# A four-layer Mamba stack with an FP4 feed-forward on one core: TensorE's work laid out anew over the slots, gates and row statistics moved off VectorE, the first norm and the weight preparation moved into the start of the Mamba block

## The chip, the cores and the metric

The kernel runs on one NeuronCore of a Trainium2 chip. The metric is the time of one execution on the device in microseconds, the median of several. Five engines work side by side and meet only at semaphores: TensorE (PE, matrix products into PSUM), VectorE (DVE), ScalarE (ACT), GpSimd (POOL, which reads and writes SBUF only) and SyncE (SP, which issues all DMAs here). Each engine takes its instructions strictly in the order in which the program lists them, so an instruction that waits holds up all behind it.

## The reference

The input x is 4 sequences of 2048 rows of 256 numbers. The layer is a residual Mamba stack of four layers, then a feed-forward with FP4 quantisation:

```python
x = x + mamba_stack(layernorm(x))        # 4 layers, below
x = x + ffn_fp4(layernorm(x))            # H=256, I=704

def mamba_layer(x):                      # D_MODEL 256, D_INNER 512, D_STATE 16
    xs, z = split(x @ in_w.T)
    xc = silu(conv4(xs) + cb)            # causal, 4 taps
    dt, B, C = split(xc @ xp_w.T)        # 16 + 16 + 16
    delta = softplus(dt @ dt_w.T + dt_b)
    h_t = h_{t-1} * exp(delta * A) + (delta * xc) * B     # 512 channels x 16 states
    y = sum_states(h_t * C) + xc * D_skip
    out = (y * silu(z)) @ out_w.T
    return layernorm(out + x) * ln_w + ln_b

def ffn_fp4(x):   # every operand quantised to E2M1 by blocks of 16
    return q(silu(q(x) @ q(w_gate).T) * (q(x) @ q(w_up).T)) @ q(w_down).T
```

All arithmetic is float32.

## The kernel before

The 8192 rows are cut into 16 chunks of 512 time steps, four chunks to a sequence. Three blocks run one after the other, with a barrier of all engines between them. `normalise_input` takes the chunks one by one: load, VectorE's statistics and normalisation, store to the buffer `xbuf` in HBM. `mamba_layers` makes 64 turns, one for each chunk of each layer (turn g is chunk g mod 16 of layer g div 16). `fp4_ffn` first quantises and transposes its weights, then goes over the chunks.

A turn has 16 slots. A slot s holds 512 of the 8192 recurrences (a group, "G" in the code): four states of one tile of 128 channels-by-states, each of them 512 time steps long. In the code of one turn each engine has its own list of what it does in slot s, and this list is the schedule:

- VectorE does four scans (`scan`, L950: h = dA * h + bu along time) and two products (`times_b`, L935: bu = durep * B_all, in PSUM). In slot s the order is scan 0, `times_b(s,1)`, scan 1, scan 2, `times_b(s+1,0)`, scan 3. So `times_b` of the next slot is the second product of this one. Between them it does the gates (`gate`, L956: sz = acc * sz, in slots 2, 6, 10 and 14, after scan 0) and the row statistics of the layer norm (`statistics` in slot 8, `moments` in slot 9).
- TensorE does `broadcast_b(s+1)` (L455, which spreads B over the partitions into the one PSUM tile `B_all`; it waits until both products of slot s have read it), then `sum_states(s-2)` (L473: the sum over states of hc into the one PSUM tile `acc`, preceded by `skip_term` when a tile of channels begins), then the projections of this slot: `project_x` in 2, `project_dt` in 3 and 4, `project_out` in 5 and 6, `project_in` of z in 8 and 9, the transposes of the chunk after next in 10, `project_in` of xs in 11 and 12, `convolve` in 13 to 15 and 0. These all pass through two PSUM tiles W0 and W1, which ScalarE empties.
- ScalarE copies the last states of slot s-1 (`keep_states`, L612, which waits for the last scan of that slot), makes the four decay factors of slot s+1 (`exp`, L603, into `dA`, a ring of 8 tiles), then does its share of the slot: `copy_conv` and `tanh_xc` and `silu_z` in 0 and 1, `copy_proj` in 3, `delta_linear` in 4 and 5, `sigmoids` in 5, `polynomial` in 6, `copy_out` in 6 and 7, `copy_z` in 9 and 10, and so on.
- GpSimd does `times_c` (L832, hc = h * C, two pairs in a slot; pair k waits for scans 2k and 2k+1, and for `acc` to have summed the pair that lay in its buffer two slots before), and as extra work `silu_xc` before slot 2, `softplus` 0 before slot 7, `softplus` 1 after slot 8, 2 after slot 10, 3 after slot 11, the layer norm's small steps in slots 10 and 12, and its weights (`affine`) after slot 15.

A channel of the next turn goes through ScalarE's `sigmoids` and `polynomial`, GpSimd's four softplus steps, a store to HBM (`store_delta`, `store_du`) and a load that repeats it over partitions (`load_delta` into `drep`, `load_du` into `durep`).

The turns are a loop of four over the middle of the 64:

```python
def turns(eng, turn):
    turn(0, 0)
    turn(1, 1)
    with eng.Fori(0, (TOT - 4) // 4) as i:
        for r in range(2, 6):
            turn(4 * i + r, r % 4)
```

In one of four turns (ph 0, the first chunk of a sequence) the scans start from zero, in the others from `carry`.

## Time and profile before

| | before |
|---|---|
| median of 3 runs | 8526.1 us (8520.08 to 8530.0) |
| profiled execution, its own time | 8524.19 us |
| span of its instructions | 8522.4 us |
| busy: VectorE | 7936.9 us, 93% |
| busy: GpSimd | 6990.0 us, 82% |
| busy: TensorE | 6497.0 us, 76% |
| busy: ScalarE | 5407.2 us, 63% |
| granted TensorE clock, mean | 0.9 |

Busy time is the union of an engine's instructions. The shares are means over three blocks with different limits. A wait row says which engine's work ended an idle time of another. In the rows below a matrix product in float32 counts as two instructions ("x2").

### The profile page before, as it was taken

The page shows a single profiled execution, that of the slowest core. Times are in us where ns is not written, and L with a number is a line of the kernel's source. Part 1 is how long each engine was busy: PE and PEld are TensorE (multiplying, and loading weights), DVE is VectorE, ACT ScalarE, POOL GpSimd, SP SyncE. Part 2 cuts the span into 40 slices and gives each one's busy share as a digit, 9 for nine tenths or more (in the row PEclk, how much of TensorE's full clock was granted, in tenths as well). Part 3 has the DMA queues.
Part 4 walks back from the last instruction along what each step waited for, and adds up shares of the span by engine and source line. Part 5 has one row for each costly group of instructions (what it writes and reads, how often), then busy time and mean ns, then how long its engine had stood idle before and what let it go on. Part 6 is the DMA issues. An engine that isn't in the chain of part 4 may idle for free. (4 is left out here: it accounts for less than half of the span.)

```text
span 8522.4 us, 96647 instructions
## 1 busy us (share of the span) xinstructions
PE 6497.0 (76%) x21028; PEld 2513.0 (29%) x21028; DVE 7936.9 (93%) x8028; ACT 5407.2 (63%) x8725; POOL 6990.0 (82%) x3390
## 2 busy tenths in 40 slices
PE   3778777777777777877778777777777777764888
PEld 1222222222222222222222222222222222221555
DVE  3999999999999999999999999999999999995777
ACT  2666666666676666667666666666666666752444
POOL 1888888888888898888888888988888888884555
PEclk9899998988998899889899898989898988986999
DMA  4455443445444544445444454544554444541110
GB/s 134 98 117 120 116 115 97 114 119 132 112 104 111 121 115 113 107 117 123 118 114 112 101 118 115 121 117 107 117 119 117 112 106 106 124 112 43 37 38 30
DMA packets 567641, 909.46 MB, mean 107 GB/s; under 512 B 58288, under 2 KB 202032, under 8 KB 565936
## 3 DMA queue, kind: packets, MB, share of 16 engines
q1 hardware_dynamic: 566960, 902.24, 44.1%
q8 instruction: 201, 3.29, 0.2%
q14 instruction: 480, 3.93, 0.2%
HBM read 715.36 MB, written 186.65 MB: 106 GB/s over the span
## 5 line engine op out<-in xcount | busy, mean ns | idle before, releaser
L832 POOL TENSOR_TENSOR hc<-h,crep 128x1024 f32<-128x1024 f32 x2048 | 4785.2, 2361 | 837.0 <-PE acc L473 755.7
L950 DVE TENSOR_TENSOR_SCAN h<-dA,carry,bu 128x512 f32<-128x512 f32 x3072 | 3769.8, 1266 | 94.3 <-issue 51.8
L935 DVE TENSOR_TENSOR bu<-durep,B_all 128x1024 f32<-128x1024 f32 x2048 | 2485.6, 1214 | 192.1 <-DMA durep<-du_dram 142.5
L603 ACT ACTIVATE dA<-drep,cur 128x512 f32<-128x512 f32 x4096 | 2618.7, 710 | 13.9 <-DMA drep<-delta_dram 13.8
L455 PE MATMUL B_all<-dtc,spread_b 128*128 128x512 f32 x2048 | 1352.2, 747 | 1646.5 <-DVE bu L935 1645.0
L612 ACT COPY carry<-h 128x4 f32<-128x4 f32 x1023 | 201.0, 197 | 2232.2 <-DVE h L950 2184.8
L473 PE MATMUL acc<-hc,gather 128*32 128x512 f32 x8192 | 1279.9, 701 | 4.4 <-POOL hc L832 4.4
L950 DVE TENSOR_TENSOR_SCAN h<-dA,bu 128x512 f32<-128x512 f32 x1024 | 1197.0, 1206 | 9.0 <-ACT dA L603 8.9
L493 PE MATMUL work<-xT,inw 128*128 128x512 f32 x2048 | 1020.2, 643 | 59.5 <-ACT xT L623 48.9
L455 PEld LDWEIGHTS B_all<-dtc,spread_b 128*128 128x128 f32 x2048 | 366.8, 212 | 2330.2 <-DVE bu L935 2266.2
L503 PE MATMUL work<-xs,taps 128*128 128x512 f32 x2048 | 965.2, 614 | 0.0
L493 PEld LDWEIGHTS work<-xT,inw 128*128 128x128 f32 x2048 | 400.6, 207 | 756.1 <-issue 652.1
L503 PEld LDWEIGHTS work<-xs,taps 128*128 128x128 f32 x2048 | 376.6, 194 | 617.6 <-issue 617.6
L531 PE MATMUL work<-outw,sz 128*128 128x256 f32 x2048 | 490.5, 383 | 0.0
L473 PEld LDWEIGHTS acc<-hc,gather 128*32 128x32 f32 x8192 | 173.0, 116 | 972.3 <-issue 686.1
L844 POOL TENSOR_TENSOR quad<-quad,xs 128x2048 f32<-128x2048 f32 x64 | 289.4, 4523 | 154.2 <-ACT quad L701 154.2
L531 PEld LDWEIGHTS work<-outw,sz 128*128 128x128 f32 x2048 | 395.6, 193 | 55.9
L837 POOL TENSOR_TENSOR xc<-xc,quad 128x2048 f32<-128x2048 f32 x64 | 290.0, 4531 | 144.8 <-ACT quad L668 144.8
L1258 PE MATMUL f_gu<-f_wguT,f_xqT 128*128 128x512 f32 (+1 forms) x768 | 341.7, 598 | 72.8 <-ACT f_xqT L1345 65.9
L462 PE MATMUL acc<-xc,skip 128*128 128x512 f32 x512 | 337.6, 749 | 0.0
L854 POOL TENSOR_TENSOR relu<-za,xc 128x2048 f32<-128x2048 f32 x64 | 290.5, 4539 | 0.1
L850 POOL TENSOR_TENSOR za<-quad,relu 128x2048 f32<-128x2048 f32 x64 | 290.0, 4531 | 0.1
(166 smaller groups left out, 6683.6 us busy)
## 6 DMA issues: line engine op xcount, KB each, us to landing
drep<-delta_dram SPq DMA_DIRECT2D x1024, 256.0 KB, 6.0
durep<-du_dram SPq DMA_DIRECT2D x1024, 256.0 KB, 6.7
crep<-c_dram SPq DMA_DIRECT2D x1024, 64.0 KB, 6.4
delta_dram<-za SPq DMA_DIRECT2D x64, 1024.0 KB, 4.3
du_dram<-relu SPq DMA_DIRECT2D x64, 1024.0 KB, 5.3
x_in<-xbuf SPq DMA_DIRECT2D x65, 512.0 KB, 3.9
x_res<-xbuf SPq DMA_DIRECT2D x64, 512.0 KB, 3.9
xbuf<-x_res SPq DMA_DIRECT2D x64, 512.0 KB, 5.6
```

The costliest lines, as they stand in the source:

```text
L455: pe.matmul(B_all[:], spread_b[:, s % QS, :], dtc[:, p_, :], start=True, stop=True).then_inc(bb_ready, 1)
L462: pe.matmul(acc[:], skip[:, q, :], xc[:, p_, q, :], start=True, stop=False, skip_group_check=True)
L473: ins = pe.matmul(acc[32 * k:32 * k + 32, :], gather[:], hc[:, 4 * (s % 2) + k, :], start=False, stop=s % QS == QS - 1, skip_group_check=True)
L493: ins = pe.matmul(W[b][:], inw[:, k, z * DI + e * P:z * DI + (e + 1) * P], xT[:, k, :], start=k == 0, stop=k == KD - 1)
L503: ins = pe.matmul(W[b][:], taps[:, 4 * e + k, :], xs[:, e, k:k + T], start=k == 0, stop=k == 3)
L531: ins = pe.matmul(half, sz[:, p_, k, t * P:(t + 1) * P], outw[:, k, :], start=False, stop=k == DB - 1)
L603: act.activation(dA[:, 4 * (s % 2) + k, :], drep[q % 2][:, k, :], ACT.Exp, scale=cur[:, p_, 4 * s + k:4 * s + k + 1]).then_inc(da_ready, 1)
L832: pool.tensor_tensor(hc[:, pair, :], h[:, pair, :], crep[:, j:j + 1, :].to_broadcast([P, 2, T]), ALU.mult).then_inc(hc_ready, 1)
L854: pool.tensor_tensor(relu[:], za[:], xc[:, p_], ALU.mult).then_inc(du_ready, 1)
L935: dve.tensor_tensor(bu[:, 2 * k:2 * k + 2, :], durep[q % 2][:, 2 * k:2 * k + 2, :], B_all[:].unsqueeze(1).to_broadcast([P, 2, T]), ALU.mul ...
L950: dve.tensor_tensor_scan(h[:, r, :], dA[:, r, :], bu[:, k, :], start, ALU.mult, ALU.add).then_inc(scanned, 1)
L1258: ins = pe.matmul(gu[:, at:at + width], xqT[:, t % 2, k, :], wguT[:, k, at:at + width], start=k == 0, stop=k == KD - 1)
```

## The change

Eight things are changed together.

1. `normalise_input` is gone as a block. Its work is done at the start of the Mamba block: all 16 chunks are loaded into tiles that are still unused (`held`), VectorE works on them in five batches, and the first chunk goes to TensorE straight from there.
2. The quantisation and transposition of the feed-forward's weights is done there too, in five pieces (`quantise_piece` on VectorE, `turn_piece`, `copy_piece`); the result is stored in HBM and loaded when the feed-forward begins.
3. The gates: ScalarE copies `acc` to SBUF (`take_sums`) after the factors in slots 2, 6, 10 and 14, and GpSimd multiplies (`gate`) after `times_c` of these slots. TensorE's next tile of sums waits for ScalarE's copy.
4. The row statistics: ScalarE's `copy_out` gives row sums, its `squares` (slot 10) sums of squares, GpSimd's `mean` (slot 8) and `variance` (slot 11) do the rest. `copy_out` is in slots 7 and 8, `root_guess` in 12, `newton_step` in 13, `normalise` in 15, `affine` after slot 0 of the next turn.
5. The ring of decay factors `dA` has 6 tiles; the other two (`sums`) hold the copies of `acc`. So factor k of slot s+1 waits for the scan six before it: factor 2 for scan 0 of slot s, factor 3 for scan 1.
6. TensorE: the skip term comes after sums, not before (`SKIP_AT`), `project_out` is in quarters over slots 5, 6 and 7 (two in 7), z's third and fourth tiles are in 9 and 10 (`copy_z` in 9, 10 and 11), the taps run in reverse.
7. All 64 turns are written out; there is no loop.
8. A constant in the work on A is changed by 3e-6.

```diff
+    SKIP_AT = (1, 0, 0, 2)
+        sums = dA[:, 6:8, :]
         def turns(eng, turn):
-            turn(0, 0)
-            turn(1, 1)
-            with eng.Fori(0, (TOT - 4) // 4) as i:
...
+            for g in range(TOT):
+                turn(g, g % 4)
             def sum_states(at, p_):
                 n, s, G = at
-                if s % QS == 0:
-                    skip_term(n, p_, s // QS)
+                q = s // QS
+                if s % QS == 0 and positive(DB * n + q):
+                    pe.wait_ge(acc_read, DB * n + q)
...
+                if s % QS == SKIP_AT[q]:
+                    skip_term(n, p_, q)
...
-                        if s in (5, 6):
+                        if s in (5, 6, 7):
                             project_out(g - 1, other, s - 5)
+                        if s == 7:
+                            project_out(g - 1, other, 3)
                     if not is_last(g):
-                        if s in (8, 9):
-                            project_in(nxt, 2 * (s - 8), 1)
-                            project_in(nxt, 2 * (s - 8) + 1, 1)
+                        if s == 8:
+                            project_in(nxt, 0, 1)
+                            project_in(nxt, 1, 1)
+                        if s in (9, 10):
+                            project_in(nxt, s - 7, 1)
@@ ScalarE
-                    if positive(4 * G + k - 7):
-                        act.wait_ge(scanned, 4 * G + k - 7)
-                    act.activation(dA[:, 4 * (s % 2) + k, :], drep[q % 2][:, k, :], ACT.Exp,
+                    if positive(4 * G + k - 5):
+                        act.wait_ge(scanned, 4 * G + k - 5)
+                    act.activation(dA[:, (4 * G + k) % 6, :], drep[q % 2][:, k, :], ACT.Exp,
+            def take_sums(n, q):
+                act.wait_ge(summed, 2 * (NG * n + QS * (q + 1)))
...
+                act.copy(sums[:, q % 2, :], acc[:]).then_inc(acc_read, 1)
+            def squares(m):
+                act.wait_ge(mean_ready, m + 1)
...
+                for t in range(NT):
+                    ins = act.activation(sums[:, t // 2, t % 2 * D:(t % 2 + 1) * D], x_res[:, t, :], ACT.Square, bias=minus_mean[:, t:t + 1],
+                                         accum_out=sq_sum[:, t:t + 1])
                 for s in range(NG):
                     keep_states(group(g, s - 1))
                     exp(group(g, s + 1), here if s + 1 < NG else other)
+                    if s == 10 and not is_first(g):
+                        squares(g - 1)
+                    if s == 2 and not is_first(g):
+                        take_sums(g - 1, DB - 1)
+                    if s in (6, 10, 14):
+                        take_sums(g, (s - 6) // 4)
@@ GpSimd
+            def gate(n, p_, q):
...
+                pool.wait_ge(acc_read, DB * n + q + 1)
+                pool.tensor_tensor(sz[:, p_, q, :], sums[:, q % 2, :], sz[:, p_, q, :], ALU.mult).then_inc(gated, 1)
                     times_c(group(g, s))
+                    if s == 2 and not is_first(g):
+                        gate(g - 1, other, DB - 1)
+                    if s in (6, 10, 14):
+                        gate(g, 1 - other, (s - 6) // 4)
...
-                        if s == 15:
-                            affine(g - 1, 0)
-                            affine(g - 1, 1)
+                    if s == 0 and isinstance(g, int) and g >= 2:
+                        affine(g - 2, 0)
+                        affine(g - 2, 1)
@@ VectorE
                     scan(at, ph, 0)
-                    if s == 2 and not is_first(g):
-                        gate(g - 1, other, DB - 1)
-                    if s in (6, 10, 14):
-                        gate(g, here, (s - 6) // 4)
                     times_b(at, 1)
                     scan(at, ph, 1)
                     scan(at, ph, 2)
                     times_b(nxt, 0)
-                    if s == 9 and not is_first(g):
-                        dve.wait_ge(stats, g)
                     scan(at, ph, 3)
-                    if not is_first(g):
-                        if s == 8:
-                            statistics(g - 1)
-                        if s == 9:
-                            moments()
```

On TensorE, slot 6 of a middle turn stands so before (the broadcast for slot 7, the skip term and sums of slot 4, two quarters of the output projection, the broadcast for slot 8; `acc_read` is given by VectorE's gate):

```order
L455 MATMUL B_all<-dtc,spread_b 128x512 [waits bu_ready]
L462 MATMUL acc<-xc,skip 128x512 [waits acc_read]
L473 MATMUL acc<-hc,gather 32x512 [waits hc_ready]
...
L529 MATMUL work<-x_res,ident 128x256 [waits w_read1]
L531 MATMUL work<-outw,sz 128x256 x4
L529 MATMUL work<-x_res,ident 128x256
L531 MATMUL work<-outw,sz 128x256 x4
L455 MATMUL B_all<-dtc,spread_b 128x512 [waits bu_ready]
```

and so in the changed kernel:

```order
L457 MATMUL B_all<-dtc,spread_b 128x512 [waits bu_ready]
L474 MATMUL acc<-hc,gather 32x512 [waits hc_ready,acc_read]
...
L462 MATMUL acc<-xc,skip 128x512
L537 MATMUL work<-x_res,ident 128x256
L539 MATMUL work<-outw,sz 128x256 x4
L457 MATMUL B_all<-dtc,spread_b 128x512 [waits bu_ready]
```

The skip term moved behind the sums, one quarter moved to slot 7, and the wait for `acc_read` stands on the first sum, between the two broadcasts as before. It is ScalarE that gives `acc_read` now, in slots 5 and 6 of its own list. Before:

```order
L682 ACTIVATE za<-work,bias_now 128x512 [waits w_filled0]
L683 ACTIVATE relu<-work,bias_now 128x512
L686 ACT_TABLE_LOAD
L689 ACTIVATE za<-za,minus_ln 128x2048 [waits w_read1,w_read0]
L691 ACTIVATE xs<-za 128x2048 [waits z_of_dt]
L692 ACT_TABLE_LOAD
L612 COPY carry<-h 128x4 [waits scanned]
L603 ACTIVATE dA<-drep,cur 128x512 [waits scanned] x4
L698 ACTIVATE quad<-xs,quad_bias 128x2048 [waits delta_ready,zz_ready]
```

and in the changed kernel, where the copy of the sums stands behind the two table loads, the two wide steps and the factors of slot 7:

```order
L716 ACTIVATE za<-work,bias_now 128x512 [waits w_filled0]
L717 ACTIVATE relu<-work,bias_now 128x512
L720 ACT_TABLE_LOAD
L723 ACTIVATE za<-za,minus_ln 128x2048 [waits w_read1,w_read0]
L725 ACTIVATE xs<-za 128x2048 [waits z_of_dt]
L726 ACT_TABLE_LOAD
L646 COPY carry<-h 128x4 [waits scanned]
L637 ACTIVATE dA<-drep,cur 128x512 [waits scanned] x4
L755 COPY dA<-acc 128x512 [waits squared,gated,summed]
L732 ACTIVATE quad<-xs,quad_bias 128x2048 [waits delta_ready,zz_ready]
```

What moved is the release of `acc`: from VectorE, after the first scan of the slot, to this place of ScalarE's list.

## Rows read from the trace of the kernel before

**Rows 1.** Busy: PE, PEld, DVE, ACT, POOL; granted clock, DMA share, GB/s; middle turns.

```profile
400.00:2400.00 2000.00, 1552.70 (x5019) 568.63 (x5016) 1944.53 (x1829) 1342.94 (x2152) 1745.64 (x797) 0.91 0.48 115
```

**Rows 2.** Waits: who waited for whom, us in total, times, longest.

```profile
DVE bu L935 <- DMA durep<-du_dram: 142.5, 36, 101.7
...
DVE h L950 <- issue: 51.8, 8, 6.7
...
DVE bu L935 <- PE B_all L455: 46.2, 78, 1.3
```

**Rows 3.** Timeline of VectorE, one slot from zero and one from carry: start, duration.

```profile
300.29 1.21 DVE L935 TENSOR_TENSOR bu<-durep,B_all 128x1024 f32<-128x1024 f32 x1
...
307.00 1.22 DVE L935 TENSOR_TENSOR bu<-durep,B_all 128x1024 f32<-128x1024 f32 x1
...
4619.90 1.21 DVE L935 TENSOR_TENSOR bu<-durep,B_all 128x1024 f32<-128x1024 f32 x1
...
4626.85 1.21 DVE L935 TENSOR_TENSOR bu<-durep,B_all 128x1024 f32<-128x1024 f32 x1
```

**Rows 4.** Timeline of VectorE, first product and last scans of the block.

```profile
214.69 1.23 DVE L935 TENSOR_TENSOR bu<-durep,B_all 128x1024 f32<-128x1024 f32 x1 [101.69 <-DMA durep<-du_dram]
...
7740.53 3.63 DVE L950 TENSOR_TENSOR_SCAN h<-dA,carry,bu 128x512 f32<-128x512 f32 x3
```

**Rows 5.** Timeline of ScalarE, slots 1, 5 and 6 of one turn.

```profile
4575.67 0.20 ACT L612 COPY carry<-h 128x4 f32<-128x4 f32 x1 [3.58 <-DVE h L950]
...
4586.23 1.28 ACT L775 ACT_TABLE_LOAD   x1
...
4604.32 0.20 ACT L612 COPY carry<-h 128x4 f32<-128x4 f32 x1 [1.99 <-DVE h L950]
...
4615.95 2.56 ACT L603 ACTIVATE dA<-drep,cur 128x512 f32<-128x512 f32 x4
4618.41 1.99 ACT L698 ACTIVATE quad<-xs,quad_bias 128x2048 f32<-128x2048 f32 x1
```

**Rows 6.** Groups by line: busy us, mean ns; then idle before.

```profile
L832 POOL TENSOR_TENSOR hc<-h,crep 128x1024 f32<-128x1024 f32 x2048 | 4785.2, 2361 | 837.0 <-PE acc L473 755.7 <-DVE h L950 79.8
...
L710 ACT COPY x_res<-work 128x512 f32<-128x512 f32 x128 | 72.2, 564 | 33.6 <-PE work L531 33.6
...
L1476 POOL TENSOR_TENSOR f_res<-f_res,f_x 128x256 f32<-128x256 f32 x60 | 44.0, 733 | 0.2 <-issue 0.2
```

**Rows 7.** Timeline of TensorE, slots 2 to 8 of that turn.

```profile
4590.23 3.70 PE L510 MATMUL work<-xc,xpw 128*128 128x512 f32 x8
...
4606.64 2.08 PE L455 MATMUL B_all<-dtc,spread_b 128*128 128x512 f32 x2 [2.91 <-DVE bu L935]
...
4614.55 1.02 PE L455 MATMUL B_all<-dtc,spread_b 128*128 128x512 f32 x2
...
4617.35 0.70 PE L529 MATMUL work<-x_res,ident 128*128 128x256 f32 x2
...
4621.78 1.02 PE L455 MATMUL B_all<-dtc,spread_b 128*128 128x512 f32 x2
...
4630.12 1.93 PE L473 MATMUL acc<-hc,gather 128*32 128x512 f32 x8
```

**Rows 8.** Timelines of GpSimd (softplus 0) and VectorE, end of one turn.

```profile
735.76 4.51 POOL L844 TENSOR_TENSOR quad<-quad,xs 128x2048 f32<-128x2048 f32 x1 [2.69 <-ACT quad L701]
...
792.86 1.23 DVE L935 TENSOR_TENSOR bu<-durep,B_all 128x1024 f32<-128x1024 f32 x1 [1.28 <-DMA durep<-du_dram]
```

**Rows 9.** Timelines: start of the kernel, of the Mamba block, of the feed-forward.

```profile
8.01 1.38 DVE L111 TENSOR_SCALAR n_x<-n_x,n_mean,n_root 128x256 f32<-128x256 f32 x4
...
112.89 1.94 PE L483 MATMUL work<-ident,x_in 128*128 128x128 f32 x8 [112.89 <-DMA x_in<-xbuf]
...
7786.06 0.06 DVE L1518 MEMSET f_minus_magic<- 128x1 f32 x1 [12.56 <-PEq L134]
...
7842.65 1.41 DVE L1506 BATCH_NORM_STATS2 f_stats<-f_xa 128x6 f32<-128x256 f32 x4 [3.87 <-POOL f_xa L1417]
```

536 lines of the change are left out of this document (308 added, 228 removed).

## The prediction, made before the changed kernel ran

> **What bounds the kernel now.** First I read the busy shares by window: in 2000 us of middle turns VectorE is busy 97%, GpSimd 87%, TensorE 78%, ScalarE 67% [rows 1]. So VectorE sets the pace. Then its timeline, for what a slot costs when nothing is late. A slot has two products and four scans, and every second product row starts one slot later: 6.71 us in turns from zero, 6.95 us in turns from carry [rows 3]. A turn of 16 slots is 107.4 or 111.2 us, on the mean 110.25 us, and 64 turns are 7056 us. The block takes 7744.2 - 214.7 = 7529.5 us from the first product to the end of the last scan [rows 4], 117.65 us a turn. The 473 us above the bare time are gates, statistics and waits. The waits are short and of three kinds: for durep, whose 142.5 us hold 101.7 us of the start; for the instruction stream at the end of the loop's body ("issue", up to 6.7 us each); for B_all, 46.2 us in 78 waits [rows 2]. The last kind is small, but it shows that the broadcast has little room, and the change acts there.
>
> **The room of the broadcast.** Slot 5 of the turn that I follow starts at about 4604.2 (ScalarE's copy follows at once [rows 5]). TensorE gets B_all back at 4606.6 [rows 7], 2.4 us into the slot; the product that needs the next broadcast starts 4.65 us into a slot (two scans and a product behind the first). Whatever TensorE has queued ahead of the broadcast must be done some 3.6 us into the slot, and what is later stops VectorE one for one.
>
> **The change part by part.**
>
> *Removed from VectorE:* gates and statistics. With every wait gone too, the 473 us would all be won: that is the most that the turns can give.
>
> *The ring of six.* Factor 3 of the next slot now waits for scan 1 of this one, which ends about 3.6 us into the slot (two scans and a product); before, it started at about 2.1 us (three of four factors that take 2.56 us together [rows 5]). So ScalarE is 1.5 us later wherever it isn't already behind.
>
> *ScalarE's copy of the sums.* I take it at 0.56 us, the copy of the same size from PSUM [rows 6]. Its size is not the point; its place is. TensorE's sums of slot 4 wait for it in TensorE's slot 6, ahead of the broadcast for slot 8. ScalarE before: slot 5 starts at 4604.3, and the factors of slot 7 start at 4615.95 [rows 5], behind two table loads and two wide steps, 11.6 us later; with 1.5 us for the ring 13.1, which is 6.2 us into slot 6. Then four factors (2.5 us) and the copy: 9.3 us into slot 6, 2.4 us into slot 7. TensorE was ready at 3.4 us into slot 6, so it idles 6 us. What it still has to do: sums and skip term, 2.8 us less the 1.0 us of the broadcast in the same stretch = 1.8 us; one quarter of the output projection, half of 4.43 = 2.2 us; the broadcast, 1.0 us [rows 7]. That is 5.0 us, and 7.4 us into slot 7 without any loss of clock.
>
> *The clock behind an idle time.* After 2.91 us of idleness the broadcast took 2.08 us in place of 1.02 us, and in slot 8 the sums 1.93 us where they take about 1 us [rows 7]: the lower of the two clock levels. The first steps after such a gap lose 1 us each, for one to three steps. I take 2.2 us a gap, bounds 0 and 3.
>
> So there are three stops of VectorE in a turn, by the same arithmetic:
>
> - A, slot 7: 7.4 + 2.2 - 4.65 = 5.0, and about 0.5 more for waits between steps: 5.5 us (bounds 3.3 and 6.5).
> - B, slot 3. ScalarE's slot 1 starts at 4575.7, its last table load ends at 4587.5 [rows 5]: 11.85, with the ring 13.4, then factors and copy 3.2: 16.6, or 2.7 us into slot 3. Behind it TensorE has the sums (1.0), project_x (3.70) and the broadcast (1.0) [rows 7]: 8.4 + 2.2 - 4.65 = 6.0 us (bounds 3.8 and 7).
> - C, slot 11. In slot 10 the four squares, which the trace doesn't show, stand between the factors and the copy. I take 2.1 us, a quarter of a wide step (1.99 us for 2048 columns [rows 5]) and a little each, between 2.0 us and 3 us. The copy comes at 4.2 + 2.1 + 0.6 = 7 us. Sums, skip term and one half of what was 3.7 us of z follow, and the transposes wait for copy_z in ScalarE's slot 11. The broadcast is done about 7.6 us into slot 11: 3.0 us (bounds 1.9 and 4).
>
> Together 14.5 us a turn, bounds 9.0 and 17.5. In slot 14 the copy is at 4.8 us and costs nothing. Over 63 turns that is 913 us (567, 1100), so the block takes 7056 + 913 = 7970 us, 440 us more than now.
>
> *GpSimd.* It is busy 1745.64 of 2000 us [rows 1], 102.7 us a turn, of which 74.8 us are times_c. Four gates come on. A product of 512 columns lies between the 0.733 us of 256 and the 2.361 us of 1024 [rows 6]; by the line between them 1.25 us each, 5.0 us a turn, and 0.5 us of small steps: 108.2 us against 110.25 us. It fits on the sum but not everywhere: softplus 0 waits for three wide steps (2 us each [rows 5]) that now stand behind the copy, and starts about 8.2 us into slot 7. From softplus 0 to the product of the next turn that needs durep it took 792.9 - 735.8 = 57.1 us [rows 8]; with a gate and small steps 58.8. That ends 67.0 us after slot 7 starts, and VectorE would be there at 8 x 6.95 + 4.65 = 60.25 us. These 6.75 us are hidden by A and C (8.5 us). If A and C weren't there they would come out; the same holds for a 2.5 us stop in slot 3, where affine after slot 0 makes silu_xc, and so project_x, late.
>
> *The loop.* At the end of each of the loop's 15 bodies the engines wait for instructions, up to 6.7 us on VectorE [rows 2]: at most 100 us of the 473 us. Written-out turns have no such place, and I count none, since the bare slot has none; if the long straight list stalled as often, 100 us would come on top, 8920 us. The Trainium skill has the rule (Runtime: NRT & Kernel Launch, Instruction fetch mechanics): prefetch is sequential, a taken branch can stall it, so full unrolling is preferred. It speaks for the change, and the loop's waits agree; what 64 turns in a straight list do, no row here shows.
>
> *The start.* The first product comes 101.8 us after TensorE's first transpose, and all of that chain stays [rows 4, 9]. The transpose waits for the 16 chunks now; the first one alone is normalised at 9.4 us [rows 9]. 9.4 + 101.8 = 111.2, and 4 us for ScalarE's waits for later batches: 115 against 214.7, so -99 us (bounds -110 and -75). Its cover: VectorE has 16 x 2.8 us of statistics and normalisation (1.41 + 1.38 us a chunk [rows 9]), an estimated 15 us of small steps, and the weights, under 56.6 us with all other engines' steps between (I take 40): some 100 us, just under the 115.
>
> *The feed-forward.* From its first instruction to its first statistics are 56.6 us [rows 9]; what stays is the load of x and one sum of 1024 columns (2.36 us [rows 6]), some 9 us by my estimate. -47 us (bounds -50 and -40).
>
> *The tail* of the block: squares for statistics and one more step on each side, +3 us.
>
> **Sum**, against the profiled execution's own 8524.2 us (the median of the runs is 8526.1, so nothing to convert): 8524.2 - 99 - 47 + 3 + 440 = 8821 us. I give 8820. With 9.0 us a turn it is 8475, with 17.5 us 9010. The stops decide the sign: at 9.8 us a turn the times are equal.
>
> **The rivals.**
>
> - *Faster (12%).* The copies come in time, because ScalarE is less behind than the rows put together say, and GpSimd keeps up: 1 us of stops a turn. 7056 + 63 - 7529.5 - 143 + 8524.2 = 7970 us. For it: VectorE is the bound at 97%, and its gates and statistics go. Against it: the trace already shows ScalarE at the factors of slot 7 only 11.6 us behind the start of slot 5, 4.7 us into slot 6, before anything is added. It decides the sign from 9.8 us a turn down.
> - *Only GpSimd's chain and durep (13%).* TensorE's wait for the copy costs little, but softplus 0 is late: 6.75 + 2.5 = 9.25 us a turn, 8490 us. For it: durep is already a wait at the end of many turns [rows 2, 8]. Against it: the sums are queued ahead of the broadcast.
> - *Worse (10%).* GpSimd at 98% of the bare turn falls behind as well (its times_c waits for the sums that wait for ScalarE), and the gaps don't overlap: 19 us a turn, 9110 us.
> - *My forecast (65%)*: 8820 us, own range 8620 to 8980.
>
> Range 8450 to 9000: it takes in the second rival and the forecast's bounds, and leaves out most of the first and the last. Three runs before lie within 10 us, so 0.2% (17 us) is about what can be told. Slower: forecast, worse rival and a little of the second, 0.76. Faster: the first rival and most of the second, 0.20. Within: 0.04.
>
> **What the new profile would show.** Right: VectorE waiting for B_all at the second product of slots 3, 7 and 11, 3 to 6 us each, some 190 long waits with 800 to 950 us; TensorE waiting for ScalarE's copy ahead of these; the first product at 115 us; the feed-forward some 690 us long; VectorE's busy share under 90%; more TensorE time at the lower clock. Wrong: waits for B_all under 200 us in total, or VectorE's longest waits on durep (second rival) or on hc (last rival); statistics or the first product later than 140 us.

## The result, and the profile of the changed kernel

| | kernel before | changed kernel |
|---|---|---|
| median of the runs, us | 8525.2 (8520.1 to 8530.0) | 9100.2 (9094.3 to 9103.2) |
| ratio, 95% interval | 1 | 1.0676 (1.0659 to 1.0693) |
| profiled execution, span us | 8522.4 | 9101.4 |
| predicted, us | | 8820 (8450 to 9000) |

The changed kernel is 6.8% slower. The direction was forecast, and the time lies 100 us above the top of the range.

I read the same views as before. First the busy shares of 2000 us of middle turns (columns as in [rows 1]):

```profile
2400.00:4400.00 2000.00, 1470.50 (x4588) 542.10 (x4588) 1722.20 (x1492) 1312.51 (x2251) 1683.26 (x812) 0.87 0.44 105
```

VectorE is busy 86%, where it was 97% [rows 1]: it lost its gates and statistics and gained more waits than these were worth. The granted clock of TensorE fell from 0.91 to 0.87. Then the waits (who waited for whom: us in total, times, longest):

```profile
POOL hc L932 <- PE acc L474: 1197.4, 463, 9.0
...
DVE bu L1057 <- PE B_all L457: 1100.5, 252, 6.3
ACT dA L637 <- DVE h L1072: 1005.4, 774, 5.6
PE acc L474 <- ACT dA L755: 941.0, 255, 6.0
```

VectorE waits 1100.5 us for the broadcast, 252 times, where it waited 46.2 us [rows 2]. 252 is four in a turn, and I had forecast three. TensorE's sums (L474) wait 255 times for ScalarE's copy (L755): this is the chain that I had described. Now one turn from carry, VectorE's stops at the second product of slots 3, 7, 11 and 13 (start, duration, in brackets the idle time before):

```profile
1062.25 1.23 DVE L1057 TENSOR_TENSOR bu<-durep,B_all 128x1024 f32<-128x1024 f32 x1 [5.82 <-PE B_all L457]
...
1095.84 1.23 DVE L1057 TENSOR_TENSOR bu<-durep,B_all 128x1024 f32<-128x1024 f32 x1 [5.51 <-PE B_all L457]
...
1127.70 1.23 DVE L1057 TENSOR_TENSOR bu<-durep,B_all 128x1024 f32<-128x1024 f32 x1 [3.95 <-PE B_all L457]
...
1144.04 1.23 DVE L1057 TENSOR_TENSOR bu<-durep,B_all 128x1024 f32<-128x1024 f32 x1 [2.33 <-PE B_all L457]
```

In the turn from zero that follows they are 6.21, 6.01, 4.75 and 2.34 us. Over all turns the waits for B_all ahead of these four products are 357.9, 345.5, 255.0 and 139.8 us, which is 5.7, 5.5, 4.05 and 2.2 us a turn. TensorE ahead of the stop in slot 7:

```profile
1080.91 1.12 PE L457 MATMUL B_all<-dtc,spread_b 128*128 128x512 f32 x2 [0.22 <-DVE bu L1057]
1087.90 1.93 PE L474 MATMUL acc<-hc,gather 128*32 128x512 f32 x8 [5.87 <-ACT dA L755]
1089.77 2.08 PE L462 MATMUL acc<-xc,skip 128*128 128x512 f32 x2
1091.63 1.06 PE L537 MATMUL work<-x_res,ident 128*128 128x256 f32 x2
1092.49 2.40 PE L539 MATMUL work<-outw,sz 128*128 128x256 f32 x8
1094.73 1.02 PE L457 MATMUL B_all<-dtc,spread_b 128*128 128x512 f32 x2
1095.68 1.07 PE L474 MATMUL acc<-hc,gather 128*32 128x512 f32 x8
1096.67 0.70 PE L537 MATMUL work<-x_res,ident 128*128 128x256 f32 x2
1097.21 1.89 PE L539 MATMUL work<-outw,sz 128*128 128x256 f32 x8
```

It is idle 5.87 us until the copy, then does sums, skip term and a quarter of the output projection, then the broadcast, and 0.1 us behind that VectorE goes on. The sums take 1.93 us where those behind the broadcast take 1.07, the ident product 1.06 against 0.70, the quarter 2.40 against 1.89, and the skip term 2.08 against the 1.12 of elsewhere: 2.7 us lost behind this idle time. The granted clock has a mean of 0.59 from 1087.9 to 1094.7 us, most of it at the lower of the two levels, and of 1.00 in the 5.3 us that follow. And ScalarE there:

```profile
1083.43 1.28 ACT L726 ACT_TABLE_LOAD   x1
1084.72 0.20 ACT L646 COPY carry<-h 128x4 f32<-128x4 f32 x1
1084.83 2.55 ACT L637 ACTIVATE dA<-drep,cur 128x512 f32<-128x512 f32 x4
1087.29 0.56 ACT L755 COPY dA<-acc 128x512 f32<-128x512 f32 x1
```

It doesn't wait in these steps; it is behind, with the table loads and wide steps of slot 5. The fourth stop, which I had not forecast, begins on ScalarE in slot 12, in three engines' rows:

```profile
1136.44 0.20 POOL L971 TENSOR_TENSOR ve<-ve,c_eps 128x4 f32<-128x4 f32 x1
...
1136.67 0.20 ACT L769 ACTIVATE lnv<-ve 128x4 f32<-128x4 f32 x1 [2.33 <-POOL ve L971]
...
1137.11 1.07 ACT L674 COPY xs<-work 128x512 f32<-128x512 f32 x2
...
1137.74 5.40 PE L500 MATMUL work<-xT,inw 128*128 128x512 f32 x8 [3.16 <-ACT xs L674]
```

The logarithm waits 2.33 us for GpSimd's variance, which stands there behind a gate, a softplus step and two products; the copies of xs are queued behind the logarithm, TensorE's next projection waits 3.16 us for them and then takes 5.40 us in place of 3.70, and the broadcast stands behind it.

The ends, to be laid beside [rows 4, 9]: first product, last scans, start and first statistics of the feed-forward:

```profile
132.83 1.23 DVE L1057 TENSOR_TENSOR bu<-durep,B_all 128x1024 f32<-128x1024 f32 x1 [7.68 <-DMA durep<-du_dram]
...
8359.41 3.61 DVE L1072 TENSOR_TENSOR_SCAN h<-dA,carry,bu 128x512 f32<-128x512 f32 x3
...
8406.95 0.06 DVE L1634 MEMSET f_minus_magic<- 128x1 f32 x1 [43.93 <-PEq L79]
...
8415.51 1.40 DVE L1622 BATCH_NORM_STATS2 f_stats<-f_xa 128x6 f32<-128x256 f32 x4 [8.38 <-POOL f_xa L1542]
```

The start gives 81.9 us (214.7 to 132.8). The block, from the first product to the end of the last scan, takes 8363.0 - 132.8 = 8230.2 us, 700.7 us more than before: 128.6 us a turn, of which 110.25 are the bare turn of the prediction. The other 18.35 us a turn are 1174 us: 1098 us are the four stops, 24 us other waits, and 52 us show as no wait (VectorE's steps and the short gaps between them take 111.1 us a turn here, not 110.25). The step to the feed-forward is 43.9 us (before 41.9), the feed-forward 694.5 us (before 736.3). Together that is 579 us more, the difference of the two spans.

### The profile page after: what moved, and what is told of

It is laid out like the page before. It is cut to its first block and busy times, and to the rows that moved or that the text cites. A ratio compares the mean times of both kernels' runs of the same rounds, so it can differ in the third digit from the quotient of the medians.

```text
span 9101.4 us, 76141 instructions
## 1 busy us (share of the span) xinstructions
PE 6684.8 (73%) x21028; PEld 2597.8 (29%) x21028; DVE 7710.2 (85%) x7155; ACT 5761.2 (63%) x9845; POOL 7299.8 (80%) x3700
## 5 line engine op out<-in xcount | busy, mean ns | idle before, releaser
L932 POOL TENSOR_TENSOR hc<-h,crep 128x1024 f32<-128x1024 f32 x2048 | 4784.0, 2358 | 1343.5 <-PE acc L474 1197.4
L1057 DVE TENSOR_TENSOR bu<-durep,B_all 128x1024 f32<-128x1024 f32 x2048 | 2476.2, 1209 | 1113.6 <-PE B_all L457 1100.5
L637 ACT ACTIVATE dA<-drep,cur 128x512 f32<-128x512 f32 x4096 | 2703.0, 713 | 1007.1 <-DVE h L1072 1005.4
L474 PE MATMUL acc<-hc,gather 128*32 128x512 f32 x8192 | 1272.0, 696 | 946.5 <-ACT dA L755 941.0
L457 PE MATMUL B_all<-dtc,spread_b 128*128 128x512 f32 x2048 | 1218.0, 679 | 855.7 <-DVE bu L1057 851.1
L500 PE MATMUL work<-xT,inw 128*128 128x512 f32 x2048 | 1111.3, 687 | 220.5 <-ACT xs L674 184.5
L510 PE MATMUL work<-xs,taps 128*128 128x512 f32 x2048 | 942.1, 603 | 0.7 <-ACT xs L674 0.7
L500 PEld LDWEIGHTS work<-xT,inw 128*128 128x128 f32 x2048 | 435.3, 223 | 938.2 <-issue 603.1
L474 PEld LDWEIGHTS acc<-hc,gather 128*32 128x32 f32 x8192 | 170.6, 114 | 1825.1 <-ACT dA L755 1225.0
L539 PE MATMUL work<-outw,sz 128*128 128x256 f32 x2048 | 538.3, 410 | 0.0
L539 PEld LDWEIGHTS work<-outw,sz 128*128 128x128 f32 x2048 | 434.0, 212 | 75.1
L462 PE MATMUL acc<-xc,skip 128*128 128x512 f32 x512 | 408.7, 891 | 0.0
L1400 PE MATMUL f_gu<-f_wguT,f_xqT 128*128 128x512 f32 (+1 forms) x768 | 346.9, 605 | 73.7 <-ACT f_xqT L1480 66.7
L517 PE MATMUL work<-xc,xpw 128*128 128x512 f32 x512 | 339.6, 822 | 12.8 <-POOL xc L943 12.8
L939 POOL TENSOR_TENSOR sz<-dA,sz 128x512 f32<-128x512 f32 x256 | 326.6, 1276 | 0.0
```

The costliest lines, as they stand in the source:

```text
L457: pe.matmul(B_all[:], spread_b[:, s % QS, :], dtc[:, p_, :], start=True, stop=True).then_inc(bb_ready, 1)
L462: pe.matmul(acc[:], skip[:, q, :], xc[:, p_, q, :], start=False, stop=False, skip_group_check=True)
L474: ins = pe.matmul(acc[32 * k:32 * k + 32, :], gather[:], hc[:, 4 * (s % 2) + k, :], start=s % QS == 0, stop=s % QS == QS - 1, skip_group_c ...
L500: ins = pe.matmul(W[b][:], inw[:, k, z * DI + e * P:z * DI + (e + 1) * P], xT[:, k, :], start=k == 0, stop=k == KD - 1)
L510: ins = pe.matmul(W[b][:], taps[:, 4 * e + k, :], xs[:, e, k:k + T], start=k == 3, stop=k == 0)
L517: ins = pe.matmul(W[0][:], xpw[:, k, :], xc[:, p_, k, :], start=k == 0, stop=k == DB - 1)
```

## The experiments

All times are medians; the kernel before ran beside each group at 8521 to 8523 us. "Per turn" is a difference of two times divided by 64. A stop's sum is that of VectorE's waits for B_all ahead of the second product of its slot, over all turns. Where rows of a wait are shown, the columns are as above.

### Undoing one thing in the changed kernel

**e1.** ScalarE's copy, and GpSimd's gate behind it, one slot earlier. The squares share the copy's tile, so they now wait for the gate of slot 9.

```diff
-                    if s in (6, 10, 14):
-                        take_sums(g, (s - 6) // 4)
+                    if s in (5, 9, 13):
+                        take_sums(g, (s - 5) // 4)
```

> The changed kernel with ScalarE's copy of the sums, and GpSimd's gate behind it, one slot earlier each (slots 1, 5, 9, 13 in place of 2, 6, 10, 14); the work is the same. Theory of the place (the copy stands behind ScalarE's late factors, TensorE's sums wait for it, the broadcast waits for them): the stops at slots 3, 7 and 11, some 15.3 us a turn, go, TensorE's wait for the copy falls from 941 us to under 100 us; what GpSimd's chain hid behind them comes out, up to 6.75 us a turn, and the stop of 2.3 us in slot 13 stays. Time 9100 - 63 x (15.3 - 6.75) = 8560 us, between 8200 (nothing comes out) and 8650. Rival, GpSimd: its four gates a turn are too much for it, and the waits only change their name (VectorE for durep or hc): over 8900 us. Rival, ScalarE as a whole is too full: the factors come late, VectorE waits for dA, over 8900 us.

8931 us, -169 where the theory said -540 (and at least -450): the direction, a third of the size, and by the time itself the rivals' case:

```profile
DVE bu L1057 <- PE B_all L457: 765.6, 164, 7.4
DVE h L1072 <- ACT dA L637: 178.4, 150, 1.4
...
ACT dA L763 <- POOL sz L939: 353.6, 63, 6.2
```

The stop at slot 7 is gone, and TensorE's sums no longer wait for the copy. But one is left at slot 3 (5 us), where GpSimd's gate now stands ahead of its product of xc and TensorE's project_x waits 290.7 us for that product (12.8 us in the changed kernel); one of 7 us is left at slot 11, because the squares (L763) wait for the gate; and VectorE now waits for factors: a copy in slot 5 stands and waits for its sums, with the factors behind it. -335 us for B_all and +164 us for dA are -171 us; measured -169.

**e5.** e1 with the squares' rows in xs, which is idle there; their wait for the gate goes.

```diff
-act.activation(sums[:, t // 2, t % 2 * D:(t % 2 + 1) * D], x_res[:, t, :], ACT.Square, ...
+act.activation(flat_xs[:, t * D:(t + 1) * D], x_res[:, t, :], ACT.Square, ...
```

> The kernel of e1 with the squares' rows written into xs, which is idle in slot 10, so that ScalarE's squares no longer wait for GpSimd's gate of slot 9. In e1 ScalarE waited 6.1 us a turn for that gate and VectorE then 7 us at slot 11. Theory of the place: that stop goes, 62 x 7 = 430 us, and of the 6.75 us a turn that GpSimd's chain hid behind it up to 5 us come out as waits for durep; the stop in slot 3 (5 us, TensorE waits there for GpSimd's product of xc) and the one in slot 13 stay. Between 8500 and 8810 us, I take 8650. Rival (GpSimd is full, each stop removed comes back in its waits): within 60 us of 8931.

8884 us, which is the rival's case (within 60 us of 8931) and outside the theory's range. The 7 us stop is gone (2.4 us are left there), but waits for B_all are still 680.2 us, those for dA 198.0 us, and ScalarE's wait for the sums rose from 105.8 to 337.4 us. TensorE's project_x waits 318.2 us for GpSimd's product of xc. So an early copy with an early gate is no cure: it moves the waits to ScalarE and to GpSimd's product of xc.

**e2.** The root's guess behind the copies of xs in slot 12.

```diff
-                    if not is_first(g):
-                        if s == 12:
-                            root_guess(g - 1)
...
                             if s in (12, 13):
                                 copy_xs(g + 2, (ph + 2) % 4, 2 * (s - 12))
                                 copy_xs(g + 2, (ph + 2) % 4, 2 * (s - 12) + 1)
+                    if s == 12 and not is_first(g):
+                        root_guess(g - 1)
```

> The changed kernel with ScalarE's logarithm and first guess of the root behind its two copies of xs in slot 12, in place of ahead of them. Theory: the 2.3 us stop in slot 13 is ScalarE's wait for GpSimd's variance, handed on through the copies of xs to TensorE and the broadcast; it goes: 62 x 2.3 = 143 us less, 8957 us, and nothing else moves. Rival (the stop is TensorE's own: four steps at the low clock behind the idle time in slot 10 and 12): within 30 us of 9100 us.

9044 us, -56 where I expected -143. The stop in slot 13 is gone, and the waits for B_all fell by 157 us, 140 of which are that stop. So the theory has the cause and the rival is out. The other half of the question was what the stop hid:

```profile
DVE bu L1058 <- PE B_all L457: 943.2, 225, 6.4
DVE bu L1058 <- DMA durep<-du_dram: 106.6, 63, 8.4
```

The waits for durep rose from 11.6 to 106.6 us, some 1.5 us at the end of each turn: GpSimd's chain from softplus to durep was just long enough. -157 + 95 = -62.

**e3.** The ring of dA eight long, the sums in a tile of their own.

```diff
-        sums = dA[:, 6:8, :]
+        sums = sb("sums", [P, 2, T])
-                    if positive(4 * G + k - 5):
-                        act.wait_ge(scanned, 4 * G + k - 5)
-                    act.activation(dA[:, (4 * G + k) % 6, :], ...
+                    if positive(4 * G + k - 7):
+                        act.wait_ge(scanned, 4 * G + k - 7)
+                    act.activation(dA[:, (4 * G + k) % 8, :], ...
```

> The changed kernel with the ring of dA eight long again and the sums in a tile of their own. My prediction gave the ring of six 1.5 us in each of the stops at slots 3 and 7 (the copy comes that much later): 3 us a turn, 190 us in all, 8910 us. If the ring's wait is slack that the late slots take back anyway: 9050 to 9100 us.

8780 us, -320, 5.0 us a turn, more than the 3 us that I had given the ring. The sums of the four stops are 245.5, 223.3, 151.4 and 185.7 us, where the changed kernel has 357.9, 345.5, 255.0 and 139.8: per turn 1.8 us off slot 3, 1.9 off slot 7, 1.6 off slot 11, and 0.7 us more in slot 13.

**e6.** Gates on VectorE again (0.665 us each): ScalarE's copies and GpSimd's gates go, nothing else changes.

```diff
                     scan(at, ph, 0)
+                    if s in (6, 10, 14):
+                        gate(g, here, (s - 6) // 4)
                     times_b(at, 1)
```

> The changed kernel with its four gates a turn on VectorE behind the first scan of slots 2, 6, 10 and 14, as before; statistics stay on ScalarE, the ring stays six long. VectorE pays 4 gates of 0.7 us, 2.8 us a turn; TensorE no longer waits for ScalarE's copy, GpSimd has 5 us a turn less. Theory: the stops at slots 7 and 11 go (9.5 us), slot 3 keeps what GpSimd's late product of xc costs (2.5 to 5 us of 6), slot 13 keeps 2.3, durep gives back 3: 128.6 - 9.5 - 2 + 2.8 + 3 = 122.9 us a turn, 365 us less: 8740 us, between 8550 and 8850. Rival (the copy is not the cause, the ring of six and the late ScalarE are): over 9000 us.

8709 us, -391, as the theory had it (8740). The waits for B_all fell from 1100.5 to 541.2 us; VectorE pays 170 us for the gates. The stop at slot 7 is gone. But the other three aren't, though no copy holds TensorE's sums: 286.5 us are left at slot 3, 124.5 at slot 11 (which the theory had gone) and 130.2 at slot 13. At slot 3 TensorE waits 175.3 us for GpSimd's product of xc.

**e14.** Normalisation in slot 14 and GpSimd's affine steps behind slot 15, as before.

```diff
-                    if s == 0 and isinstance(g, int) and g >= 2:
-                        affine(g - 2, 0)
-                        affine(g - 2, 1)
+                    if s == 15 and not is_first(g):
+                        affine(g - 1, 0)
+                        affine(g - 1, 1)
```

> The changed kernel with the normalisation in slot 14 and GpSimd's affine steps behind slot 15, nothing else. On e7 this place was worth 227 us. In the changed kernel ScalarE's copy at slot 2 holds TensorE as long as GpSimd's product of xc does, so that here it should be hidden: theory 0 to 80 us less, 9060 us. Rival (the stop at slot 3 is GpSimd's product of xc and not the copy): 200 us and more less, under 8900 us.

9099 us, no change, and the stops of the same turn are the same to 0.02 us: 5.83, 5.52, 3.96, 2.31. So the affine steps' place isn't what sets the stop at slot 3 here: what it costs lies wholly under what else holds TensorE there. It doesn't follow that the stop is the copy's alone, since in e6, without the copy, most of it stays.

**e16.** The copy ahead of the four factors of its own slot (and the squares in xs, as in e5, because the copy of slot 10 now stands ahead of them).

```diff
                     keep_states(group(g, s - 1))
+                    if s in (6, 10, 14):
+                        take_sums(g, (s - 6) // 4)
                     exp(group(g, s + 1), here if s + 1 < NG else other)
-                    if s in (6, 10, 14):
-                        take_sums(g, (s - 6) // 4)
```

> The changed kernel with the copy ahead of the four factors of its slot, and the squares' rows written into xs (the copy of slot 10 would otherwise wait for squares that stand behind it); ring of six, affine steps, root and gates as in the changed kernel. Theory (late copy): the stops at slots 7 and 11 each lose the factors' 2.6 us and what the gap costs in clock, that of slot 3 loses less, since GpSimd's product of xc is late there as well; slot 13 stays, some durep comes out: 5 to 6.5 us a turn, 8740 us, between 8600 and 8850. Rival (the copy then waits for the sums, and VectorE for the factors, as in e8): over 8900 us.

8762 us, -338 us, 5.3 us a turn, for ScalarE's reaching four copies of 0.56 us each 2.6 us sooner. The sums of the four stops are 251.3, 130.1, 152.9 and 149.4 us: 3.4 us a turn off slot 7, 1.7 off slot 3, 1.6 off slot 11. (The squares' new place has little part in this: in the changed kernel ScalarE waits 0.4 us ahead of them in the whole run.)

### Everything undone but one

**e7.** e6, e3, e2 and e14 together: the gates, the ring, the root's guess and the affine steps are in their old places or lengths, the rest of the change stays.

> As e6, and with the ring eight long, the root's guess behind the copies of xs, the normalisation in slot 14 and GpSimd's affine steps behind slot 15 (before's places). Theory: no long wait for B_all is left; a turn is 110.25 + 2.8 and some 2 us of rest, 115 us: 8230 us, between 8150 and 8400, under both kernels. Rival (GpSimd's chain from softplus to durep sets the turn): waits for durep of 3 us a turn and more, 8400 to 8500 us.

8301 us, ratio 0.974 (0.9723 to 0.9756): faster than both kernels.

```profile
2400.00:4400.00 2000.00, 1566.78 (x5111) 568.25 (x5109) 1950.80 (x1728) 1400.16 (x2434) 1786.11 (x829) 0.93 0.49 115
```

```profile
DVE bu L1045 <- PE B_all L457: 73.7, 106, 3.3
DVE bu L1045 <- DMA durep<-du_dram: 70.8, 64, 8.0
```

VectorE is back at 97.5%, and a turn takes (7549.7 - 133.0) / 64 = 115.9 us (expected 115; from the profiled execution, 13 us shorter than the median). This kernel has no stop at slot 7 or 13, and 35.3 and 37.4 us in all at slots 3 and 11. From it GpSimd's gates (e9), the ring of six (e10) and the affine steps' place (e11) were put back by themselves, and the copy on ScalarE on top of e9 (e13). The root's guess was not.

**e9.** As e7, but VectorE only copies the sums (0.666 us) and GpSimd makes the gates (1.279 us).

```diff
-dve.tensor_tensor(sz[:, p_, q, :], acc[:], sz[:, p_, q, :], ALU.mult).then_inc(acc_read, 1)
+dve.tensor_copy(sums[:, q % 2, :], acc[:]).then_inc(acc_read, 1)
```

> The kernel of e7, but VectorE only copies the sums out of acc (slots 2, 6, 10, 14, in the place of its gates) and GpSimd makes the four gates from the copy; the squares go into xs. It differs from e7 by GpSimd's four gates alone, 1.26 us each. Theory that only the copy's place matters: GpSimd has room (108 of 115 us a turn), at most 1 us a turn comes out: 8300 to 8370 us. Rival (GpSimd is the second bound, as e8 hints: what it takes on comes out in waits for hc, durep and xc): 3 to 5 us a turn, 8490 to 8620 us.

8432 us, 2.1 us a turn more, between theory and rival. VectorE's cost is the same, so this is GpSimd's gates (with the squares' rows in xs, whose part wasn't taken apart):

```profile
DVE bu L1044 <- PE B_all L457: 134.1, 121, 4.3
DVE h L1059 <- POOL hc L921: 126.4, 66, 3.0
```

**e13.** e9 with the copy on ScalarE in its places of the changed kernel.

```diff
-                dve.tensor_copy(sums[:, q % 2, :], acc[:]).then_inc(acc_read, 1)
+                act.copy(sums[:, q % 2, :], acc[:]).then_inc(acc_read, 1)
```

> The kernel of e9 with the four copies on ScalarE, behind its factors in slots 2, 6, 10 and 14, the changed kernel's places; nothing else differs from e9 (8432 us). Theory (the late copy holds TensorE's sums, and those the broadcast): stops at slots 3, 7 and 11 of some 3 to 4 us each as in e3, partly on top of what e9 has: 3.5 us a turn more, 8650 us, between 8560 and 8760. Rival (the ring, GpSimd's gates and its affine steps were the whole of it, the copy itself is nearly free): within 50 us of 8432.

8775 us, 5.4 us a turn more than e9, although VectorE does 170 us less; that is 15 us above the theory's range. This is the copy's move to ScalarE, behind the factors, and nothing else. It is the dearest of the four things put back:

```profile
DVE bu L1055 <- PE B_all L457: 665.7, 201, 5.6
...
PE acc L474 <- ACT sums L754: 628.2, 188, 5.5
```

201 waits, three a turn, at slots 3, 7 and 11 (288.2, 237.4 and 131.6 us, in e9 103.7, 0 and 27.7): the three that I forecast, without the fourth.

**e15.** e13 with the copy ahead of the factors of its slot (the edit of e16).

> The kernel of e13 with the copy ahead of the four factors of its slot. ScalarE reaches it 2.6 us earlier. Theory (late copy): each stop of slots 3, 7 and 11 is up to 2.6 us shorter, 3 to 7 us a turn less than e13, and VectorE waits less than 1 us a turn for dA: 8450 us. Rival (as in e8, where the copy stood a slot earlier: ScalarE then waits for the sums and the factors behind it come late): not faster than e13, with VectorE's waits for dA over 100 us.

8505 us, 4.2 us a turn less than e13: ratio 0.9981 (0.9971 to 0.9990). TensorE's wait for the copy fell from 628.2 to 204.3 us and VectorE's for B_all from 665.7 to 269.6 us; for dA VectorE waits 24.4 us, and for GpSimd's hc 145.3 us (37.2 in e13). So of e13's 5.4 us a turn 4.2 are the place behind the factors. A turn takes 119.3 us here, 9.0 above the bare one, at which the prediction's break-even (9.8) says just under the kernel before; so it is.

**e8.** The kernel of e13 with ScalarE's copies and GpSimd's gates one slot earlier.

> The kernel of e5 (copies and gates one slot earlier, squares into xs) with the ring of eight, the root's guess behind the copies of xs, the normalisation in slot 14 and GpSimd's affine steps behind slot 15. Theory: no long wait for B_all is left, VectorE has nothing beside products and scans, and a turn is the 110.25 us and 3 to 5 us that GpSimd's chain to durep gives: 8180 us, between 8080 and 8350, the fastest of all. Rival (GpSimd with four gates is full at 108 us a turn and falls behind at its affine steps): over 8400 us, and slower than e7.

8830 us, the rival: 56 us slower than e13, 325 us slower than e15.

```profile
DVE bu L1055 <- PE B_all L457: 373.7, 190, 4.4
DVE h L1070 <- ACT dA L637: 194.4, 122, 2.8
DVE h L1070 <- POOL hc L932: 174.6, 103, 3.0
...
ACT sums L754 <- PE acc L474: 498.0, 195, 8.2
```

ScalarE waits 498 us for sums that aren't there yet, and its factors are late instead. The gates are early too: TensorE's project_x waits 236.2 us for GpSimd's product of xc, which now stands behind a gate (11.8 us in e13). What the early copy alone would cost, no run shows. Of the three places tried the middle one is the best: e8 is ahead of it, e13 behind it, e15 in it.

**e10.** e7 with the ring six long (the edit of e3 undone).

> The kernel of e7 with the ring of dA six long. My prediction gave the ring 1.5 us in each late slot, hidden where ScalarE isn't late; e3 gave 5 us a turn with the copy in ScalarE's chain. Without the copy: 1 to 2 us a turn if only a late ScalarE makes the ring cost, 8370 to 8430 us. Rival (the ring costs by itself, VectorE waits for dA): 4 us a turn and more, over 8550 us.

8482 us, 2.8 us a turn, between the two. B_all 254.0 us against 73.7, and this at slots 3 (124.1 us) and 11 (127.5 us): the likely way is that later factors make ScalarE's answers to TensorE later, copy or not. VectorE itself waits little for dA (60.7 us).

**e11.** e7 with the affine steps behind slot 0 of the next turn and the normalisation in slot 15.

> The kernel of e7 with the normalisation in slot 15 and GpSimd's affine steps behind slot 0 of the next turn, as in the changed kernel. Theory: the two steps, 9.2 us, stand just ahead of GpSimd's product of xc, TensorE's project_x waits for it and VectorE for the broadcast at slot 3: 2.5 us a turn as predicted, up to 4: 8460 us, between 8400 and 8560. Rival (GpSimd has caught up by slot 2 either way): within 30 us of e7.

8528 us, 3.5 us a turn, and all of it at slot 3, where VectorE waits 271.7 us, 3.6 to 5.9 us a turn: TensorE's project_x waits 204.7 us for GpSimd's product of xc, in e7 59.3 us.

### The loop and the start

**e4.** The kernel before, its 64 turns written out one after the other.

```diff
-            with eng.Fori(0, (TOT - 4) // 4) as i:
-                for r in range(2, 6):
-                    turn(4 * i + r, r % 4)
+            for g in range(TOT):
+                turn(g, g % 4)
```

> The kernel before with its 64 turns written out one after the other, nothing else changed. The loop's part was bounded at 100 us by the waits for instructions at the end of the loop's 15 bodies: between 8425 and 8525 us. If part of the loss of the changed kernel comes from the long straight list of instructions, this one is slower than 8525 us, by up to 100 us.

8435 us, ratio 0.9895 (0.9878 to 0.9911), -87 us of at most 100. VectorE's waits for instructions (51.8 us [rows 2]) are gone, and those for dA fell from 44.6 to 2.7 us: together 93.7 us. The straight list costs nothing that can be seen.

**e12.** The changed kernel with GpSimd's first softplus step held until VectorE has two pieces of the weights done.

```diff
+                    if n == 0:
+                        pool.wait_ge(piece_ready, 2)
                     pool.wait_ge(lin_ready, n + 1)
```

> The changed kernel with GpSimd's first softplus step of the start held until VectorE has two pieces of the weights done. In the changed kernel VectorE's steps of piece 1 beside GpSimd's wide products took 3.7 to 5.0 us in place of 0.2 to 1.2 us. Theory: they take 0.2 to 1.3 us now, piece 1 is done some 14 us earlier, the softplus steps start some 7 us later, store_delta leaves earlier than 105.9 us, and the first product stands between 122 and 130 us in place of 132.8; in all 0 to 10 us off the whole. Rival (these lengths come from something else, as the SP queue or the transfers): they stay over 3 us and the first product is later than 133 us.

9095 us (two runs; the 5 us are within the spread of the changed kernel's), and the first product at 128.64 us, 4.2 us earlier. VectorE's steps of piece 1 in the changed kernel, GpSimd beside them, and the same VectorE steps in e12:

```profile
79.25 4.52 POOL L950 TENSOR_TENSOR quad<-quad,xs 128x2048 f32<-128x2048 f32 x1 [30.61 <-ACT quad L735]
...
80.08 3.74 DVE L1140 TENSOR_SCALAR fp_scale<-fp_max 128x64 f32<-128x64 f32 x1
83.85 4.57 DVE L1142 TENSOR_SCALAR fp_nudged<-fp_scale 128x64 f32<-128x64 f32 x1
88.45 0.55 DVE L1144 RECIPROCAL fp_rec<-fp_nudged 128x64 f32<-128x64 f32 x1
89.04 4.98 DVE L1146 TENSOR_TENSOR h<-h,fp_rec 128x1024 f32<-128x1024 f32 x1
94.05 4.87 DVE L1148 TENSOR_SCALAR h<-h 128x1024 uint32<-128x1024 uint32 x1
```

```profile
80.37 0.20 DVE L1142 TENSOR_SCALAR fp_scale<-fp_max 128x64 f32<-128x64 f32 x1
80.60 0.20 DVE L1144 TENSOR_SCALAR fp_nudged<-fp_scale 128x64 f32<-128x64 f32 x1
80.83 0.55 DVE L1146 RECIPROCAL fp_rec<-fp_nudged 128x64 f32<-128x64 f32 x1
81.42 1.22 DVE L1148 TENSOR_TENSOR h<-h,fp_rec 128x1024 f32<-128x1024 f32 x1
```

They are short now; the long ones moved to piece 2, where the softplus steps went, so that VectorE's weights take 54 us here as well.

## Why the prediction was right in direction and too low

**The main step was right.** ScalarE's copy, behind its factors, holds TensorE's sums and through them the broadcast. e13 against e9 changes only the engine of the copy and shows it at 343 us; e15 and e16 show that 270 and 338 us come back when the copy stands ahead of the factors, the second in the changed kernel itself. Its arithmetic held closely. The copy of slot 6 was to end 2.4 us into slot 7 and ended 2.2 us into it (slot 7 would start at 1095.84 - 5.51 - 4.65 = 1085.7, the copy ends at 1087.85); that of slot 10 was to come at 7 us and came at 6.9.

**But the copy isn't the only cause at slots 3 and 11.** Only the stop of slot 7 goes whole with it (e6). At slot 3, where e7 has 35 us, the affine steps' place alone makes 272 us (e11), the ring alone 124 us (e10), and the copy adds 184 us to e9; at slot 11 the ring alone makes 127 us. In the changed kernel they lie over each other and give 358 and 255 us, so that undoing one there gives less than its price, or nothing (e14). The prediction had this for the affine steps; for the ring it had only a delay of the copy.

**The step that failed is the sum of the stops: 913 us, and it is 1174.** It took three stops where there are four, putting slot 13 at nothing, and made stop C too small. Term by term, us over the 63 turns that the prediction counts, per turn in brackets:

| stop | predicted | measured |
|---|---|---|
| A, slot 7 | 346 (5.5) | 345.5 (5.5) |
| B, slot 3 | 378 (6.0) | 357.9 (5.7) |
| C, slot 11 | 189 (3.0) | 255.0 (4.05) |
| slot 13 | 0 | 139.8 (2.2) |
| all else above the bare turn | 0 | 76 (1.2) |
| sum | 913 (14.5) | 1174 (18.6) |

- *The stop in slot 13 was missed.* I wrote that in slot 14 the copy costs nothing, which is right, and went through no other wait of ScalarE's that TensorE hangs on. GpSimd's variance, which stands behind more of GpSimd's work (for the squares themselves it waits only once in 64 turns), was late for the logarithm, and the copies of xs are behind that. e2 shows the cause; it also shows that the place was worth only 56 us by itself, since durep was next in line.
- *C was 1.05 us a turn too small.* The copy was where I put it. Behind it the sums, the skip term and one half of z took 1.94 + 2.07 + 2.58 us where they take 1.07, 1.12 and 1.88 at the higher level: 2.5 us in place of the 2.2 taken. The rest lies in what follows, the transposes with their waits, for which the prediction shows no figure.
- *Together* these two are 206 of the 261 us by which the stops were too small (8230 against 7970 us for the block). A and B were 21 us less than forecast, and 76 us are the last row: 24 us of other waits and the 52 us by which a turn without waits is longer than the 110.25 us that four rows gave.
- *The range* fell with it: its top of 9000 us is that of three stops at their upper bounds (17.5 us a turn, 9010 us), and no bound had room for a fourth.

**The clock.** Taken at 2.2 us a gap between 0 and 3, measured 2.7 in slot 6 (granted 0.59) and 2.5 in slot 10 (0.58). A mean clock of 0.87 where 0.91 stood before fits. That A came out at 5.5 us has some luck in it: it held 0.5 us for waits between steps, of which the rows show none, and that is just what the gap was too small by. No kernel here had the gaps at the higher level, so what they would cost then is not shown.

**The ring.** Given 1.5 us in each of the stops of slots 3 and 7; e3 took 1.8 and 1.9 us a turn from these and 1.6 from slot 11, which I had not counted, 5.0 us a turn over the whole. I had it as part of the late copy only; e10 shows that it costs 2.8 us a turn with no copy on ScalarE.

**GpSimd.** The gate was 1.276 us (1.25 taken; the line between the two rows gives 1.276) and the sum of its work fitted (108.2 us a turn forecast and measured). What comes out when the copy is out of the way was priced at 6.75 us for durep and 2.5 us for the affine steps. The affine place cost 3.5 us (e11), and, as the prediction said, nothing while the stop at slot 3 covers it (e14). Durep cost 1.0 to 1.6 us a turn (e2, e7, e13), far less than 6.75. In e7 the chain from softplus 0 to the product that needs durep is 57.4 us (1577.95 to 1635.39), of the length that I had; but softplus 0 starts 6.1 us into slot 7 there (the slot starts at 1571.9), not 8.2, and the product comes later by two gates and by 2.9 us of other waits. The 8.2 us held 1.5 us for the ring and 0.6 for the copy, and I had kept these while taking the stops away. The rival "only GpSimd's chain" was priced too high by that; no run has late softplus steps without the stops, so its own case stays untested.

**The loop.** At most 100 us, counted as won with the bare turn; e4 measured 87. The Trainium skill's rule that a taken branch can stall prefetch (Runtime: NRT & Kernel Launch, Instruction fetch mechanics) holds here in its direction, with that number.

**The start, 17 us too good** (-82 against -99). The first transpose came at 9.99 us (9.4 forecast). The chain behind it took 122.8 us where 101.8 and 4 for ScalarE's waits were taken: softplus 0 comes 6.6 us later in it than before, and then 12.9 us more pass until delta is stored (at 105.88 us, though GpSimd had it done at 92.94). SP's queue holds that store behind two loads of weights, and these wait for TensorE's turning of the pieces ahead of them, which waits for VectorE, whose weights took 55 us (70.2 to 125.2) where I took 40, 16 of them in the steps that e12 shows. In e12 the store of delta leaves at 102.60 us, at once behind GpSimd's step, and the first product is 4.2 us earlier; but its softplus steps start 8.7 us later by the experiment's own wait, so the full price of the queue isn't shown.

**The feed-forward and the tail** were within 6 us together: the way to the first statistics gave 48 us (47 forecast), the whole feed-forward 42, the step ahead of it cost 2 (3 forecast). 8821 + 260 + 17 + 5 - 1 = 9102, the profiled execution's own time of 9103 but for rounding.

**The rivals.** "Worse" (19 us a turn, 9110 us) had the number, but not the mechanism: GpSimd does wait for the sums for 1197.4 us, but VectorE waits for GpSimd's hc only 2.9 us in all. It is the forecast's own chain with one link more.

## What to carry to other kernels

A step that frees a buffer should be costed by where its engine is when the step comes up, not by its own length: against a copy on VectorE (e9), the same 0.56 us copy cost 343 us behind four factors, 73 us ahead of them, and, with GpSimd's gate moved as well, about 400 us a slot too early. When the work of one engine is taken over by others, go through every wait of the engine that feeds the bound (here each thing that TensorE has queued ahead of the broadcast), and not only through those that the change names; the fourth stop was in that list. And a stop hides the next: undo one at a time in the slow kernel, and put back one at a time in the fast one, because the two give different prices (the affine place 0 and 227 us, the ring 320 and 181 us).

## What the runs showed of the hardware

- Some of VectorE's steps on SBUF are held until a GpSimd product beside them ends. In the start a VectorE step of 64 columns took 4.57 us and one of 1024 columns 4.87 to 4.98 us while GpSimd ran products of 2048 columns of 4.5 to 5.4 us each (the step of 64 columns ended at 88.42, the product at 88.36); apart from them the same steps took 0.20 and 0.69 to 1.23 us (e12), and the reciprocal between them took 0.55 us either way. The Trainium skill states this as an exclusive lock of the port pair that the two share, not a split of bandwidth (SBUF — State Buffer, SBUF: two separate sides), and the ends agree. The products and scans of the turns, which take one operand from PSUM, keep their 1.2 us beside GpSimd's products.
- A sum that ScalarE makes on the side costs a second instruction: each of the squares is 0.49 us and a read of the accumulator 0.19 us. Four of them take 2.06 us (1116.29 to 1118.35), as the estimate of 2.1 had it.
